# Indirect DMAs held in groups of four in place of two, and the edge scans at earlier steps

## The reference

```
h    = (x @ W_gat).reshape(M, 4, 4)                       # a row of 24 numbers a node, with a_src and a_dst
e    = leaky_relu(a_src[src] + a_dst[dst])                # src, dst: 262,144 edges
ee   = exp(e - segment_max(e, dst)[dst])
agg  = segment_sum(h[src] * ee) / segment_sum(ee) + b_gat # per destination node
g    = softmax of the two best of layernorm(agg) means    # gates of four experts
out  = x + sum over experts of g * (gelu(x @ W1 + b1) @ W2 + b2)
```

## Time and profile before

| | |
|---|---|
| median of 3 runs | 4110.96 us (4102.31 to 4111.44) |
| the profiled execution | 4108.94 us, of which the span is 4107.1 us |
| POOL busy | 2458.7 us (60% of the span), 2473 instructions |
| VectorE (DVE) busy | 2243.7 us (55%) |
| TensorE (PE) busy | 1929.5 us (47%), granted clock 0.751 on average |
| ScalarE (ACT) busy | 1168.6 us (28%) |
| DMA | 247.91 MB, 60 GB/s over the span |

### The profile page before, as it was taken

One profiled execution on the slowest core, in us unless ns is written; L12 is line 12 of the kernel. 1 busy time (PEld: TensorE's weight loads), 2 busy tenths in 40 slices (PEclk: granted clock), 3 DMA queues, 4 the chain that ended last, 5 costly groups with the idle time before them and its releaser, 6 DMA issues.

```text
span 4107.1 us, 29248 instructions
## 1 busy us (share of the span) xinstructions
PE 1929.5 (47%) x7631; PEld 843.2 (21%) x7631; DVE 2243.7 (55%) x3946; ACT 1168.6 (28%) x1734; POOL 2458.7 (60%) x2473
## 2 busy tenths in 40 slices
PE   0442129899786868686640546774752000000034
PEld 0111113333232323232210212332321000000023
DVE  8888988888667676767766425544020120210345
ACT  0210005556443434343320424453642000000000
POOL 1000007567777667676777777767777777777573
PEclk9965559999998989898865777897976555555567
DMA  4110005544443434344233222232332111101134
GB/s 106 25 25 0 0 15 94 84 85 84 79 69 80 76 76 80 77 70 78 48 66 35 62 51 69 62 85 66 112 91 68 27 27 10 27 10 26 38 111 123
DMA packets 652075, 247.91 MB, mean 60 GB/s; under 512 B 552277, under 2 KB 632709, under 8 KB 649477
## 3 DMA queue, kind: packets, MB, share of 16 engines
q1 hardware_dynamic: 573988, 216.76, 22.5%
q0 software_dynamic: 77920, 29.29, 7.0%
HBM read 152.68 MB, written 91.71 MB: 60 GB/s over the span
## 4 chain that ended last, share of the span: by engine, by line
DMA 47%; POOL 15%; issue 13%; PE 10%; DVE 9%; DVEq 5%; ACT 1%; POOLq 0%; SPq 0%; ACTq 0%
DMA ring<-table,src_i 44%; POOL ring L785 13%; DVE res L1293 5%; DVEq L1295 5%; DMA ring<-partial,ends_i 2%; PE ps L882 2%; PE ps L872 1%; PE ps L897 1%; PE ps L1047 1%; DVE res L1294 1%; POOL adst_d L762 1%; PE ps L923 1%; PE ps L931 0%; PE ps L874 0%; PE ps L842 0%
## 5 line engine op out<-in xcount | busy, mean ns | idle before, releaser
L785 POOL DMA_INDIRECT ring<-table,src_i x2048 | 2020.3, 986 | 793.3 <-issue 440.6
L1597 DVE TENSOR_TENSOR_SCAN ad<-ns,cad,raw 128x128 f32<-128x128 f32 (+2 forms) x68 | 26.5, 452 | 938.5 <-DMA ring<-table,src_i 938.4
L751 POOL DMA_INDIRECT ring<-keys_d,place x128 | 141.6, 1106 | 644.7 <-DVEq L1250 592.4
L986 PE MATMUL ps<-arena 64*128 64x512 f32 x800 | 222.8, 680 | 454.4 <-DMA arena<-xnT 250.0
L1033 PE MATMUL ps<-ident,ends 128*20 128x128 f32 x6 | 1.5, 418 | 758.1 <-DVEq L1829 758.1
L882 PE MATMUL ps<-arena,w 64*128 64x448 f32 x896 | 249.9, 637 | 174.2 <-DVE arena L1640 108.1
L1106 ACT ACTIVATE ex<-ex 128x1024 f32<-128x1024 f32 (+2 forms) x17 | 17.1, 1006 | 1039.4 <-DVE ex L1612 1039.4
L1181 ACT ACTIVATE arena<-ps,arena 128x1024 f32<-128x1024 f32 x200 | 213.3, 1115 | 118.5 <-PE ps L986 118.4
L897 PE MATMUL ps<-arena,w 128*64 128x448 f32 x896 | 215.3, 603 | 41.6 <-issue 41.6
L1640 DVE TENSOR_TENSOR arena<-arena,ps 128x448 f32<-128x448 f32 x297 | 172.3, 617 | 111.4 <-ACT ps L1100 111.3
L1100 ACT ACTIVATE ps<-ps,tb 128x448 f32<-128x448 f32 x297 | 169.6, 605 | 199.0 <-PE ps L882 178.3
(11 more groups left out here) (338 smaller groups left out, 3914.1 us busy)
## 6 DMA issues: line engine op xcount, KB each, us to landing
arena<-in_x SPq DMA_DIRECT2D x304, 110.0 KB
ring<-table,src_i POOLq DMA_INDIRECT x2048
partial<-res SPq DMA_DIRECT2D x15, 1536.0 KB, 6.1
arena<-in_x SPq DMA_DIRECT2D x160, 140.0 KB
outputs_d<-arena SPq DMA_DIRECT2D x32, 512.0 KB
arena<-outputs_d SPq DMA_DIRECT2D x32, 512.0 KB, 5.0
arena<-xnT SPq DMA_DIRECT2D x100, 128.0 KB, 3.4
arena<-h_tok SPq DMA_DIRECT2D x50, 256.0 KB
```

The costliest lines, as they stand in the source:

```text
L785: g.indirect_dma_start(out=ring[k % 2][:, j - FROM[k], :], out_offset=None, in_=table[0:GRAPH_NODES, :], in_offset=off(ap=src_i[:, j:j + 1 ...
L986: m = mm(hid[ee % 2][:, z * NT:(z + 1) * NT], fw1[lower_upper(z), ee, :], xf[q][lower_upper(z), :], start=True, stop=True)
```

## The change

Three constants change, nothing else. `GROUP` goes from two to four, so POOL waits before every fourth indirect DMA and not before every second, for the group of four that lies two groups in front. This holds for the search, the scatters, the gathers and the node gathers. The scans 1 to 5 move to earlier front steps, scans 8 to 10 move to earlier pairs, and scan 11, which stood behind the last pair, now stands behind pair 42.

```diff
-SCAN_AFTER_STEP = {31: 0, 37: 1, 43: 2, 49: 3, 54: 4, 59: 5}
-SCAN_AFTER_PAIR = {0: 6, 8: 7, 20: 8, 31: 9, 41: 10}
-GROUP = 2
+SCAN_AFTER_STEP = {31: 0, 36: 1, 41: 2, 46: 3, 51: 4, 57: 5}
+SCAN_AFTER_PAIR = {0: 6, 8: 7, 13: 8, 22: 9, 33: 10, 42: 11}
+GROUP = 4
```

## The result

The kernel with the change takes 3968.89 us (median of 4 runs, 3965.88 to 3981.61), beside 4109.21 us for the kernel before in the same comparison (4 runs). The ratio is 0.9665, with a 95% interval of 0.9649 to 0.9682: 3.4% less. 3970 us was forecast.

A forecast was written before the change was run, and what follows sets the result against it. POOL's issue rate was taken to bound the kernel from first gather to last. Span 4107.1 - 134 - 1 - 6 = 3966 us, profiled execution 3968, median 3970 us; range 3950 to 4010, 8 in 10.

The forecast's parts named there:

- (1): Holds of the 2048 gathers: 142 us of waiting less 8 us left at stores, 134 us less, between 107 and 142.
- The rule of 3.0 and 5.5 us after a start: Gather holds: POOL stops only for landings later than 3.0 us after start with groups of two, 5.5 with four.
- (2): Descriptor making (986 ns on average) and the 16 pauses inside groups of gathers are not touched: 0 us.
- (3): Search 0 us, as POOL waits for the turned places; scatters 1 us, between 0 and 2, then the front's pace limits.
- (4): Node gathers (L800): 6 us less, between 0 and 8, through DVE's shorter wait up to the third batch.
- (5): Moved scans: each 57 to 85 us ahead of its need, cost 0; old places would cost some 10 us of gain.
- No wait removed: Rival on gather holds: landings are always early, idle time is POOL's own, about 4111 us; 3 in 100.
- The delay comes back: Rival on the front's late landings: more DMAs in flight only land later, 4033 us (3995 to 4060); 10 in 100.
- Scans hold the gathers: Rival: gathers wait for `scan_used` because the front or scan slots fall late, 10 to 30 us, 3980 to 4000; 4 in 100.
- Slower by descriptor making: Rival on POOL: more open DMAs lengthen descriptor making; from 66 ns each the 141 us are lost again; 4 in 100.
- The pauses go too: Rival: the 16 pauses inside groups of gathers shrink as well, 27 us more, 3943 us; 5 in 100.
- The fixed landing time of the Trainium skill: Rule for one gather DMA: 2.0 us plus bytes at 436 GB/s, 2.03 us, so no hold waits; about 4111 us.

## Why the prediction was right, point by point

**Where the time is.** POOL's issue rate set the time from the first gather to the last, before and after. The start (1024.6 us) and the last gather (3724.1 us, forecast 3717) bear it out, and PE's wait of 577.8 us (forecast 575), which begins at 3159.5 us (forecast 3155), shows how far the other engines are from it.

**Why a hold waits, (1).** The loss at holds went from 140.5 to 9.4 us, 131 us less, where 142 - 8 = 134 were forecast. The rule of 3.0 and 5.5 us after a start fits every variant: fifteen of the 16 long losses go with the stores made small, a reach of five DMAs leaves what landings of up to 7.3 us explain (8.1 us in the kernel with groups of two), and a reach of nine leaves nothing. The experiments also show what it is not: groups of two that look three groups in front bring nearly the same as groups of four, the number of holds brings nothing, and the scans alone bring nothing.

**What is not touched, (2).** The pauses stayed, fifteen of them and 28.0 us (before sixteen and 28.4). Descriptor making took 989 ns on average and not 986: 5.7 us more over 2048, a term I had set to 0. The other kernels' groups of four say 987 to 990 ns and the groups of two 986 to 990, so at most 1 or 2 ns belong to the change and the rest is scatter of single executions. It is most of the difference between the last gather's 3724 us and the 3717 us forecast.

**Search, scatters and start, (3).** The first gather starts 1.5 us sooner (1 us forecast). That agreement tells little, since this start lies between 1023.8 and 1028.8 us in the other kernels with groups of two, and between 1020.9 and 1029.1 us in those with groups of four. The losses in the search went to DVE's wait, as said.

**Node gathers, (4).** 5.3 us up to the third batch in the changed kernel's profile, some 4 us up to the end in the comparison of all kernels with node gathers in twos and in fours; 6 were forecast. DVE's third wait is 8.59 us and not near 5, because the gain lies in two waits. The second batch's went from the 18.04 us below, of the kernel before, to 14.92 us, and the third's from 11.40 to 8.59, 5.9 us together:

```profile
3954.11 0.35 DVE L1888 TENSOR_TENSOR arena<-ring,arena 128x128 f32<-128x128 f32 x1 [18.04 <-DMA ring<-partial,ends_i]
```

The profiled execution lost this again to PE and ACT in the fourth batch. No other kernel's profile has that, so I take it for an accident of this execution, which was not tested.

**Scans, (5).** Scans 0 to 5 end at 1318, 1480, 1643, 1804, 1967 and 2134 us (forecast 1319, 1480, 1642, 1803, 1965, 2135), chunks 2 to 7 start at 1375, 1545, 1715, 1885, 2053 and 2226 us (forecast 1376 to 2220, at most 8 us off). No gather waits for a scan. At the old places one does, for 6.8 us, scan 3 as worked out; scan 4, for which 4 us were expected, is in time. The old places cost 7 us by the medians and by that one wait, where 10 were forecast.

**The sum.** The profiled span went from 4107.1 to 3979.8 us, 127.3 us less: 131.1 at the holds, 0.4 at the pauses and 1.5 at the start, less 5.7 of longer descriptor making and nothing from the tail. The forecast of 3966 us for the span is 14 us under this one execution: 7.5 us up to the last gather, most of it the descriptor making and 3 us at the holds, and 6 us in the tail. The three others took 3965.88 to 3969.64 us, and the median is 1 us from the forecast. The mechanism and the large term are borne out, but that the sum agrees to 1 us is in part luck: the four runs spread over 16 us, and the median to which the forecast added its terms moved by 1.8 us with the fourth run of the kernel before.

**The rivals.** No wait removed: fell, 131 us went. The delay comes back: fell, with more DMAs in flight the latest landing that stopped POOL came 7.3 us after its start (7.7 before), and none stopped it away from a store. Scans hold the gathers: fell for the new places and is seen once at the old ones. Slower by descriptor making: fell, 3 ns and not 66. The pauses go too: fell for this change, but the 27 us that it put on them are real, as the kernels with three semaphores show. "They don't stand at groups" was right and yet no reason to leave them out of reach: what removed them is a change in how many semaphores take turns and how far the hold looks. The fixed landing time of the Trainium skill (DMA: Bandwidth & Descriptors, "Anatomy of one DMA — SWDGE (gpsimd) path") would have meant no change; the 131 us that went decide against it wherever a store or the front's traffic runs beside the gathers.

## What to carry to other kernels

Where an engine issues small DMAs behind holds, compare the time since the awaited DMA's start with the latest landing beside the largest transfer, and not with a landing in quiet: here 3.75 us of reach cost 140 us, 6.25 us cost 9, and 11.2 us nothing, while the holds themselves were free. Sum the idle time beyond the usual gap and sort it by where it stands, ahead of a group or inside one; what stands inside a group is of another cause, and may be worth an experiment of its own, such as one more semaphore, which gave 28 us here with groups of four. When the bound engine gets faster, write down when each hand-placed consumer must be done before and after: the places that were free before cost 6.8 us afterwards.

## What was not expected of the hardware

**A pause once in 128 indirect DMAs.** With two semaphores in turn POOL stands for about 2 us (3.2 at most in the changed kernel's gathers) once in 128 indirect DMAs. Each kind is counted from its own start, and the pause stands ahead of the 114th: 113 DMAs of the search lie before the first of the rows below, 113 scatters before the second, 113 gathers before the third and 113 + 13 x 128 = 1777 gathers before the fourth. Counted over all kinds together the second and the third are 119 DMAs apart and the third and the next one 138, so it is no count over the whole queue:

```profile
768.19 0.95 POOL L751 DMA_INDIRECT ring<-keys_d,place  x1 [1.65 <-issue]
...
1015.63 0.97 POOL L762 DMA_INDIRECT adst_d<-res,place  x1 [1.68 <-issue]
...
1175.89 0.95 POOL L785 DMA_INDIRECT ring<-table,src_i  x1 [3.24 <-issue]
...
3375.14 0.95 POOL L785 DMA_INDIRECT ring<-table,src_i  x1 [1.93 <-issue]
```

Groups of two, four and eight have it alike (28.4, 28.0 and 30.0 us over the gathers), and so does the kernel with twice the holds (28.9 us), so the holds don't move it. With three or four semaphores for the gathers and groups of four the gathers have none, while the two in the search and the scatters, which kept two semaphores, stay. With groups of two and three semaphores it is all but gone at a reach of three groups (1.0 us in sum) and 0.45 us shorter at a reach of two. What it is, and why it depends on the semaphores, stays open.

**A landed hold is free.** Twice as many holds left L785's idle time at 660.5 us (661.9 with half of them) and the kernel's time at 3968.9 us.

**A large load beside the gathers.** With the stores made small, the one long hold left stands behind SyncE's load of all graph nodes' rows, 3.12 us of idle time for a gather that landed 5.8 us after its start. Store and load together stood beside the latest landing of all, 8.1 us. That the load delays the gathers as a store does was not tested by itself.

**One run out of line.** One run of the kernel with groups of two and a reach of three took 4698.59 us, 725 us above the five others. It has no profile, and it is not explained.
